# Half-row matmuls in pairs and a new order of pieces for the softmax maxima of a cross-attention

## The chip, the cores and the metric

The kernel runs on one core of a Trainium2 chip. The metric is the device time of one execution in microseconds (us). Five engines work side by side and meet at semaphores: TensorE (PE in the profile; its weight loads, PEld, overlap its matmuls), the vector engine (DVE), ScalarE (ACT), GpSimd (POOL), and SyncE (SP), whose queue issues the transfers.

## The reference

A decoder layer for 32 batches of 56 tokens of width 128: a self-attention whose softmax runs over the queries, a cross-attention to 1500 context rows of width 96 per batch, and a mixture of 8 experts with the two best chosen per token. Each part is followed by a residual sum and a layer norm. The change lies in the cross-attention:

```
q = (query @ Wq + bq)  -> 16 heads of 8
k = (key_value @ Wk + bk), v = (key_value @ Wv + bv)
attn = softmax(clip(q @ k^T * 8**-0.5, -10000, 10000))     # 16 heads x 56 queries x 1500 keys
x = (attn @ v) @ Wo + bo
```

## The kernel before, in words

The self-attention and the setup take the first 70 us or so, then a loop over the 32 batches does the cross-attention, and from some 768 us on the experts run. The change touches the loop and the part ahead of it that prepares batches 0 and 1.

**One batch in the loop.** The scores are computed transposed: keys in the partitions, 896 = 16 x 56 columns of head and query in the free dimension. The 1500 keys are cut into 12 chunks of 125, and the loop has one slot c per chunk (`period`, lines 1576 to 1665 for TensorE, 998 to 1063 for the vector engine, 748 to 778 for ScalarE). In a slot TensorE makes the scores of chunk c (line 1590: 4 matmuls into banks 2 and 3 or 4 and 5), ScalarE takes their exponentials (line 759), and TensorE later multiplies these by the values into bank 6 (lines 1655 and 1659: 4 + 4 matmuls with 25 and 9 columns of weights, at partitions 0, 32, 64 and 96 of the output; each matmul of plain fp32 leaves two records). `OUTPUTS` names the slots in which the outputs of which chunks are made: 2 in slot 2, 3 in slots 5 and 8, 1 in slot 10, 3 in slot 11.

**The maxima.** A softmax needs the maximum over all keys of each row before the first exponential. It is made one or two batches ahead, from rounded keys `K_hi` and block-diagonal queries `Q_bd` (head h has its 8 rows 8h to 8h+7, and zeros in the others). Rows of 16 heads x 56 queries make 7 groups of 128 (RG = 7), the keys 3 thirds of 500 (NB = 3): 21 *pieces* per batch, each one matmul of 128 rows, 128 columns of weights and 500 columns (`piece`, line 1403, matmul at 1414) into bank 0 or 1 by `bank_of(n)`, and one maximum over 500 numbers by the vector engine (`piece_max`, line 941, at 946). Piece n is group n // 3, third n % 3. With two banks, piece n waits until piece n - 2 is reduced (line 1413). When all 21 are done, `row_max` (954) takes the maximum of the three thirds, TensorE turns it into a row (`turn`, 1431, slot 8), `row_out` (961) writes its negative, and SyncE's queue moves it into the last row of the next batch's stacked queries.

**The order.** It is written out by hand in tables from slot to pieces: `EARLY_PIECES` stand right behind the slot's scores, `MID_PIECES` behind the projections of slot c and ahead of the outputs, `LATE_PIECES` behind the outputs. Pieces 0 to 8 belong to the batch after next, 9 to 20 to the next (`pieces`, line 328). The vector engine takes early and mid pieces first in a slot, then `row_max` in slot 7, `row_out` in slot 8, the reciprocals of the softmax sums in slots 0 and 1 (line 1013), the scaling of the outputs in slot 5 (line 1018), then late pieces. In TensorE's queue a slot holds: scores, early pieces, the sums of the batch before (slot 0, line 1545), a third of the values of a later batch (slots 9, 11 and 3, line 1421), a third of its keys (slots 5, 6 and 8, line 1426), mid pieces, the turn (slot 8), outputs, late pieces. Each engine runs its queue strictly in the order written; ahead of the loop the pieces of batch 0 and the first 9 of batch 1 are listed by `pieces0` and `pieces1`.

Of the kernel before, what the change touches and what calls it, by code (L numbers as in the profile page):

```python
# [24 lines left out]
AX = mybir.AxisListType  # L25
# [14 lines left out]
KB = 500  # L40
NB = NK // KB
# [12 lines left out]
SUM_SLOT, TURN_SLOT = 0, 8  # L54
V_COPIES = (9, 11, 3)
K_COPIES = (4, 6, 7)
EARLY_PIECES = {0: (9,), 1: (10,), 2: (11,), 3: (12,), 4: (14,), 6: (18,), 7: (20,), 9: (2,), 10: (4,), 11: (6,)}
MID_PIECES = {3: (13,), 5: (15, 16), 6: (19,), 8: (0,), 9: (3,), 11: (7,)}
LATE_PIECES = {5: (17,), 8: (1,), 10: (5,), 11: (8,)}
OUTPUTS = {2: (0, 1), 5: (2, 3, 4), 8: (5, 6, 7), 10: (8,), 11: (9, 10, 11)}  # L60
NP = 3
P_AT, T_AT, X_AT, LOGITS_AT = 3, 5, 9, 11
# [6 lines left out]
RG = HQ // 128  # L69
HG = H // 4  # L70
PIECES = RG * NB
SUM = 0
V3, V1 = 3 * DH + 1, DH + 1
VC = 4 * (V3 + V1)
# [2 lines left out]
PRIME = 4  # L77
# [8 lines left out]
def decoder_kernel(nc, gate_rows, x1_rows, xT, x, ctx_in, wq, wk, wv, xWq, xbq, xWk, xbk, xWv, xbv, xWo, xbo, Wr, W1, W2, out):  # L86
    stack = ExitStack()

    def sb(name, shape, dt=F32):
        return stack.enter_context(nc.sbuf_tensor(name, shape, dt))  # L90

    def sem(name):
        return stack.enter_context(nc.semaphore(name))

    with stack:
# [30 lines left out]
        K_hi = sb("K_hi", [128, 2, NK], F32R)  # L126
        K_st = sb("K_st", [128, 2, HG, NK], F32R)
        Q_st = sb("Q_st", [DC + 1, 2, HG, 4, S], F32R)
        Q_bd = sb("Q_bd", [128, 2, H, S], F32R)
# [9 lines left out]
        def at(parts, *shape, place=None):  # L139
            n = math.prod(shape)  # L140
            o = used[0]
            used[0] += n
            place = whole if place is None else place
            assert used[0] <= place.shape[-1], used[0]
            v = place[0:parts, o:o + n]
            if len(shape) == 2:
                v = v.rearrange("p (a b) -> p a b", b=shape[1])
            elif len(shape) == 3:
                v = v.rearrange("p (a b c) -> p a b c", b=shape[1], c=shape[2])
            return v  # L150

        Qs_all = at(DC, HG, B * S)
        start = used[0]
# [22 lines left out]
        def held(u):  # L176
# [15 lines left out]
        mx = at(128, RG, NB)  # L192
# [107 lines left out]
        F = {n: sem("f_" + n) for n in (  # L300
            "keys_made", "keys_copied", "keys_high", "keys_low",
            "values_made", "values_copied", "queries_spread", "stacked_spread", "max_scores_made",
            "piece_max_taken", "row_max_taken", "extremes_kept", "max_transposed", "max_row_ready",
            "scores_made", "weights_ready", "outputs_made", "outputs_copied", "sums_spread", "sums_inverted",
            "outputs_scaled", "ones_ready", "bank_cleared", "bad_ready", "bad_summed",
            "flag_ready")}
# [25 lines left out]
        def bank_of(n):  # L332

            return bank[0 if n == 0 else (n + 1) % 2]

        def has(b, ahead):

            return not isinstance(b, int) or 0 <= b + ahead < B
# [116 lines left out]
        def _(pool):  # L455
# [3 lines left out]
            def step(ins):  # L459
                ended[0] += 1  # L460
                ins.then_inc(pool_step, 1)
                pool.wait_ge(pool_step, ended[0])

            def keep(t, pattern, base, mult, op=ALU.is_ge, fill=0.0):
                step(g.affine_select(out=t, in_=t, pattern=pattern, compare_op=op, fill=fill, base=base,
                                     channel_multiplier=mult))
# [12 lines left out]
            for par in range(2):  # L479
                step(g.memset(V2[par][:, :, 0:4 * V3].rearrange("p c (m r) -> p c m r", r=V3)[:, :, :, SUM], 1.0))  # L480
                step(g.memset(V2[par][:, :, 4 * V3:VC].rearrange("p c (m r) -> p c m r", r=V1)[:, :, :, SUM], 1.0))
            for s in range(SLOTS - 1):
# [7 lines left out]
            for a3 in range(3):  # L490
                step(g.tensor_copy(four_heads[32 * a3:32 * a3 + 32, :], head_rows[32 * a3:32 * a3 + 32, 4 * a3:4 * a3 + 4]))
            keep(sum_rows[:].rearrange("p (g c) -> p g c", c=32), [[-32, 4], [0, 32]], -SUM, 1, ALU.not_equal, 1.0)
            pool.sem_inc(consts, 1)
# [3 lines left out]
            def later_constants():  # L497
# [18 lines left out]
                for g4 in range(4):  # L516
                    keep(sum_row[:], [[0, 1]], -SUM - 32 * g4, 1, ALU.not_equal, 1.0)
                pool.sem_inc(consts, 1)
# [14 lines left out]
            def spread_queries(b, par):  # L533

                g.tensor_tensor(Q_bd[:, par], Qt_all[:, bass.ds(b * S, S)].unsqueeze(1).to_broadcast([128, H, S]),  # L535
                                head_rows[:].unsqueeze(2).to_broadcast([128, H, S]), ALU.mult).then_inc(F["queries_spread"], 1)
# [33 lines left out]
            def period(b, par, half):  # L570
                if has(b, 2):
                    pool.wait_ge(F["max_scores_made"], (b + 1) * PIECES + PRIME)
                    spread_queries(b + 2, par)
# [64 lines left out]
        def _(act):  # L638
# [109 lines left out]
            def period(b, par, half):  # L748
                for c in range(NC):
# [13 lines left out]
                    if c in K_COPIES and has(b, 2):  # L763
                        n = K_COPIES.index(c)
                        act.wait_ge(F["max_scores_made"], (b + 1) * PIECES + PRIME)
                        act.wait_ge(D_[f"khi{par}"], (half + 1) * (16 * 2 * HG))
# [81 lines left out]
        def _(dve):  # L848
            v = nc.vector
# [43 lines left out]
            def first_attended(n):  # L893

                dve.wait_ge(X_[n], 16)
                dve.wait_ge(S1["outputs_made"], n + 1)
                y = firsts[n].xq
                for t in range(QT):
                    last = v.scalar_tensor_tensor(y[:, t, :], bank[2 + n % 2][0:TT, D * t:D * t + D], quads3[n].ri[:, t:t + 1], y[:, t, :], ALU.mult, ALU.add)
                last.then_inc(S1["residual_added"], 1)  # L900
                dve.wait_ge(S1["residual_added"], n + 1)
                statistics(S1, quads3[n], lambda t: y[:, t, :], tie(0), True)
# [38 lines left out]
            def piece_max(b, n):  # L941

                dve.wait_ge(F["max_scores_made"], b * PIECES + n + 1 + PRIME)
                if n == 0 and (not isinstance(b, int) or b >= 1):
                    dve.wait_ge(F["row_max_taken"], b + PRIME)
                v.reduce_max(mx[:, n // NB, n % NB:n % NB + 1], bank_of(n)[:, 0:KB], AX.X).then_inc(F["piece_max_taken"], 1)  # L946

            def row_max(b):

                dve.wait_ge(F["piece_max_taken"], (b + 1) * PIECES + PRIME)  # L950
                if not isinstance(b, int) or b >= 1:
# [23 lines left out]
            for n in range(8):  # L975
                piece_max(0, n)
            first_attended(3)
            for n in range(8, PIECES):
                piece_max(0, n)
            row_max(0)  # L980
            row_out(0)
            for n in range(3):
                piece_max(1, n)
# [14 lines left out]
            def period(b, par, half):  # L998
                for c in range(NC):
                    taken(b, c, EARLY_PIECES)  # L1000
                    taken(b, c, MID_PIECES)
                    if c == 7 and has(b, 1):
# [11 lines left out]
                    if c == 5 and has(b, -1):  # L1014
                        dve.wait_ge(F["sums_inverted"], 2 * b + PRIME)
                        if isinstance(b, int) and b == 1:
                            dve.wait_ge(D_["qr"], 16 * 3 * HG)
                        v.scalar_tensor_tensor(OS_all[:, :, bass.ds((b - 1) * S, S)], O_sb.rearrange("p (s q) -> p s q", s=SLOTS), 1.0,
                                               R_sb.rearrange("p (s q) -> p s q", s=SLOTS), ALU.mult, ALU.mult, accum_out=chk_all[:, bass.ds(b - 1, 1)]).then_inc(F["outputs_scaled"], 1)
                    taken(b, c, LATE_PIECES)  # L1020
                    P, norms = passes[0], passes[0].base3["rstd_ready"]
# [245 lines left out]
            with dve.If(clamped > 0):  # L1267
# [8 lines left out]
                with dve.Fori(0, B) as i:  # L1276
# [6 lines left out]
                    for j in range(G2):  # L1283
                        n = i * G2 + j
# [48 lines left out]
        def _(pe):  # L1333
            t_ = nc.tensor
            mm = t_.matmul
# [67 lines left out]
            def piece(b, par, n, turns):  # L1403

                if n == 0:
                    pe.wait_ge(F["queries_spread"], b + 1 + PRIME)
                if n < NB:
                    pe.wait_ge(F["keys_high"], b * NB + n + 1 + PRIME)
                if n == 2:
                    if turns:  # L1410
                        pe.wait_ge(F["max_row_ready"], b + PRIME)
                elif not (isinstance(b, int) and b == 0 and n == 0):
                    pe.wait_ge(F["piece_max_taken"], b * PIECES + (1 if n == 1 else n - 1) + PRIME)
                mm(bank_of(n)[:, 0:KB], Q_bd[:, par].rearrange("p h q -> p (h q)")[:, 128 * (n // NB):128 * (n // NB) + 128],  # L1414
                   K_hi[:, par, (n % NB) * KB:(n % NB) * KB + KB], start=True, stop=True).then_inc(F["max_scores_made"], 1)

            def value_project(par, n):

# [157 lines left out]
            def period(b, par, half):  # L1576
                for c in range(NC):
# [15 lines left out]

                    max_scores(b, par, c, EARLY_PIECES)
                    if c == SUM_SLOT and has(b, -1) and has(b, 0):
# [37 lines left out]
                    if c in K_SLOTS and has(b, 2):  # L1633
# [6 lines left out]
                        key_project(par, n, bank[7])  # L1640
                    max_scores(b, par, c, MID_PIECES)
                    if c == TURN_SLOT and has(b, 1):
                        turn(b + 1)
                    if has(b, 0):
                        for k in OUTPUTS.get(c, ()):
# [15 lines left out]
                            last.then_inc(F["outputs_made"], 1)  # L1661
                    max_scores(b, par, c, LATE_PIECES)
                    if isinstance(b, int) and b == B - 2 and c == 8:
# [83 lines left out]
            with pe.If(clamped > 0):  # L1747
                pe.wait_ge(second, 1)
                with pe.Fori(0, B) as i:
# [13 lines left out]
                    for j in range(G2):  # L1763
                        n = i * G2 + j
                        pe.wait_ge(S2["max_ready"], n + PRIME)
                        for c in range(NB):
                            last = mm(bank[c][0:TT, 0:KB], Qbd[:, 2 * j:2 * j + 2, :].rearrange("p h q -> p (h q)"), KT[:, KB * c:KB * c + KB],
                                      start=True, stop=True)
# [94 lines left out]
```

## Time and profile before

| | |
|---|---|
| median of 3 runs | 981.94 us (979.5 to 982.6) |
| span of the profiled execution | 981.2 us (the page gives no other time of that execution) |
| TensorE busy | 934.3 us (95%) |
| vector engine busy | 737.5 us (75%) |
| ScalarE busy | 647.0 us (66%) |
| GpSimd busy | 350.3 us (36%) |
| mean granted TensorE clock | 0.978 of full speed |

The rows further down are lines of the profile's page and of questions to its trace. A line of a group of instructions has the line of the kernel (L1414), the engine, the operation, output <- inputs, shapes and count, then busy time, mean duration and the idle time ahead with what ended it. A line of the chain or the timeline begins with its start and its length in us.

### The profile page before, as it was taken

To read this page: it belongs to the slowest core of one execution; us is meant where nothing else is said; L and a number is where in the kernel's file an instruction comes from. 1 tells how busy PE (TensorE), PEld (TensorE's weight loads), DVE (VectorE), ACT (ScalarE), POOL (GpSimd) and SP (SyncE) were. 2 spreads that over 40 slices of the span, in tenths; PEclk is the share of its full clock that TensorE was granted. 3 is DMA by queue.
4 is the path that set the end of the run, shared out by engine and by line. 5 is a ranking of instruction groups with operands and counts; after the bars stand their busy time and mean duration, and the time that the engine had idled before them with its cause. 6 is when DMAs were issued, how large, how long until landed. Compare 5 with 4: busy or idle time off the path is not lost.

```text
span 981.2 us, 28874 instructions
## 1 busy us (share of the span) xinstructions
PE 934.3 (95%) x10535; PEld 753.6 (77%) x10535; DVE 737.5 (75%) x1426; ACT 647.0 (66%) x1081; POOL 350.3 (36%) x334
## 2 busy tenths in 40 slices
PE   6877999999999999999999999999999899999995
PEld 4645787877777777787777877778777678999894
DVE  6673777777777777777777777777788857777996
ACT  3654777777777777777777777777776444445554
POOL 6452352223233332222323333222231413112992
PEclk8897999999999999999999999999999899999998
DMA  6538566666555556666655555666654201002331
GB/s 140 116 75 197 119 143 135 145 136 138 131 118 118 118 125 138 140 136 137 136 128 118 118 118 128 140 138 137 138 121 96 66 1 44 23 22 83 130 113 41
DMA packets 43626, 111.45 MB, mean 114 GB/s; under 512 B 15491, under 2 KB 26053, under 8 KB 43461
## 3 DMA queue, kind: packets, MB, share of 16 engines
q1 hardware_dynamic: 43572, 110.77, 49.9%
q8 instruction: 30, 0.49, 0.2%
q14 instruction: 24, 0.19, 0.1%
HBM read 32.23 MB, written 1.89 MB: 35 GB/s over the span
## 4 chain that ended last, share of the span: by engine, by line
PE 90%; DVE 4%; ACT 2%; SPq 2%; issue 1%; DMA 1%; POOL 0%; ACTq 0%; DVEq 0%
PE psum L1590 18%; PE psum L1414 18%; PE psum L1655 13%; PE psum L1421 8%; PE psum L1426 8%; PE psum L1659 4%; PE psum L1682 3%; PE psum L1683 2%; PE psum L1684 2%; PE psum L1695 2%; PE psum L1694 2%; PE psum L1696 2%; PE psum L1545 1%; PE psum L1431 1%; SPq L395 1%
## 5 line engine op out<-in xcount | busy, mean ns | idle before, releaser
L946 DVE TENSOR_REDUCE arena<-psum 128x1 f32<-128x500 f32 x672 | 443.0, 671 | 176.9 <-PE psum L1414 176.7
L759 ACT ACTIVATE arena<-psum 125x896 f32<-125x896 f32 x384 | 348.1, 916 | 114.2 <-PE psum L1590 102.5
L1414 PE MATMUL psum<-K_hi,Q_bd 128*128 128x500 f32 x672 | 310.0, 470 | 7.0 <-DVE arena L946 4.2
L547 POOL TENSOR_TENSOR arena<-arena,K_hi 128x500 fp32r<-128x500 f32 x96 | 119.9, 1249 | 407.3 <-ACT K_hi L690 407.3
L1590 PE MATMUL psum<-Q_st,K_st 97*125 97x224 f32 x1536 | 243.7, 281 | 0.7 <-ACT arena L759 0.6
L1590 PEld LDWEIGHTS psum<-Q_st,K_st 97*125 97x125 f32 x1536 | 222.7, 190 | 23.1 <-issue 3.9
L1414 PEld LDWEIGHTS psum<-K_hi,Q_bd 128*128 128x128 f32 x672 | 128.2, 191 | 64.9 <-issue 27.1
L1655 PE MATMUL psum<-arena 125*25 125x168 f32 x3072 | 171.2, 313 | 0.2
L813 ACT ACTIVATE K_st<-psum 128x448 fp32r<-128x448 f32 x128 | 69.7, 544 | 79.2 <-PE psum L1684 77.7
L1659 PE MATMUL psum<-arena 125*9 125x56 f32 x3072 | 117.7, 214 | 0.0
L1659 PEld LDWEIGHTS psum<-arena 125*9 125x9 f32 x3072 | 94.5, 92 | 16.7
L1426 PE MATMUL psum<-arena,WkA 97*128 97x500 f32 x192 | 99.0, 597 | 7.3 <-ACT arena L688 7.2
L1421 PEld LDWEIGHTS psum<-WvA,arena 97*125 97x125 f32 x768 | 99.8, 189 | 3.8
L1421 PE MATMUL psum<-WvA,arena 97*125 97x128 f32 x768 | 100.4, 274 | 0.0
L1655 PEld LDWEIGHTS psum<-arena 125*25 125x25 f32 x3072 | 69.5, 104 | 34.1 <-issue 32.9
L1071 DVE SCALAR_TENSOR_TENSOR K_st<-psum,K_st 128x448 fp32r<-128x448 f32 x128 | 76.8, 615 | 12.2 <-ACT K_st L813 11.5
L688 ACT COPY arena<-psum 128x500 f32<-128x500 f32 x96 | 55.5, 578 | 44.8 <-PE psum L1426 34.9
L540 POOL TENSOR_TENSOR Q_st<-arena,four_heads 96x896 fp32r<-96x896 f32 x32 | 53.7, 1677 | 55.4 <-PE psum L1590 55.4
L703 ACT COPY arena<-psum 125x384 f32<-125x384 f32 x96 | 46.6, 486 | 33.9 <-PE psum L1421 33.9
L690 ACT CAST K_hi<-arena 128x500 fp32r<-128x500 f32 x96 | 58.5, 610 | 3.1
L1013 DVE RECIPROCAL arena<-psum 128x112 f32<-128x112 f32 x64 | 53.8, 842 | 1.4 <-PE psum L1545 1.4
L535 POOL TENSOR_TENSOR Q_bd<-Qt_all,head_rows 128x896 fp32r<-128x896 f32 x32 | 54.1, 1690 | 0.5 <-PE psum L1414 0.5
(250 smaller groups left out, 1052.4 us busy)
## 6 DMA issues: line engine op xcount, KB each, us to landing
K_st<-K_hi SPq DMA_DIRECT2D x256, 187.5 KB, 4.7
K_st<-arena SPq DMA_DIRECT2D x128, 187.5 KB, 3.4
arena<-in_ctx SPq DMA_DIRECT2D x32, 562.5 KB, 6.7
arena<-gate_rows SPq DMA_DIRECT2D x8, 896.0 KB, 4.4
arena<-in_L_ffn_W SPq DMA_DIRECT2D x16, 256.0 KB, 3.1
Q_st<-max_row SPq DMA_DIRECT2D x224, 0.5 KB, 1.7
arena<-OS_all SPq DMA_DIRECT2D x12, 168.0 KB, 4.1
x_rows<-x_all SPq DMA_DIRECT2D x1, 896.0 KB, 6.5
```

What stands on the lines that cost most here:

```text
L547: g.tensor_tensor(low.bitcast(F32R), low, K_hi[:, par, n * KB:n * KB + KB].bitcast(F32), ALU.subtract).then_inc(F["keys_low"], 1)
L690: a.copy(K_hi[:, par, n * KB:n * KB + KB], K_lo[:, n * KB:n * KB + KB]).then_inc(F["keys_high"], 1)
L759: a.activation(P2[c % NP].rearrange("p (n k) -> p n k", n=2), psum[0:CK, 2 + 2 * (c % 2):4 + 2 * (c % 2), 0:HQ // 2], ACT.Exp)\
L813: a.activation(h_hi[u % 2][:, f], bank[f][:, 0:QC], ACT.Relu).then_inc(S4["hidden_high"], 1)
L946: v.reduce_max(mx[:, n // NB, n % NB:n % NB + 1], bank_of(n)[:, 0:KB], AX.X).then_inc(F["piece_max_taken"], 1)
L1071: v.scalar_tensor_tensor(h_lo[k % 2][:, f], bank[f][:, 0:QC], 0.0, h_hi[k % 2][:, f].bitcast(F32), ALU.max, ALU.subtract)\
L1414: mm(bank_of(n)[:, 0:KB], Q_bd[:, par].rearrange("p h q -> p (h q)")[:, 128 * (n // NB):128 * (n // NB) + 128], K_hi[:, par, (n % NB) * KB ...
L1421: last = mm(bank[7][0:CK, 128 * k:128 * k + 128], ctxT2[:, par, CK * q:CK * q + CK], WvA[:], start=True, stop=True)
L1426: mm(into[:, 0:KB], WkA[:], ctxT2[:, par, n * KB:n * KB + KB], start=True, stop=True).then_inc(F["keys_made"], 1)
L1590: last = mm(bank[2 + 2 * (c % 2) + g // 2][0:CK, 4 * S * (g % 2):4 * S * (g % 2) + 4 * S], K_st[0:DC + 1, par, g, c * CK:c * CK + CK], Q_s ...
L1655: mm(bank[6][32 * m:32 * m + V3, 0:3 * S], values[:, k, V3 * m:V3 * m + V3], weights_[:, 3 * S * m:3 * S * m + 3 * S], start=(k == 0), sto ...
L1659: last = mm(bank[6][32 * m:32 * m + V1, 3 * S:4 * S], values[:, k, 4 * V3 + V1 * m:4 * V3 + V1 * m + V1], weights_[:, (12 + m) * S:(13 + m ...
```

## The change

Two things change. The pieces that need only one half of the array's rows use only that half: groups 0 to 2 have all of their heads in rows 0 to 63, groups 4 to 6 in rows 64 to 127, and group 3 lies across both and keeps all 128 rows. And the order is new: `PIECE_ORDER` goes through the thirds of the keys one after the other, within a third a lower and an upper half follow each other, and the slot tables put most pieces in twos right behind the scores. For the pieces of groups 0 to 2 and 4 to 6 the pairs that stand next to each other in the loop are 1 and 2, 3 and 4, 5 and 6, 7 and 8, 9 and 10, 11 and 12, 14 and 15, 16 and 17, 18 and 19; the whole-array pieces 0, 13 and 20 stand alone. A pair's two matmuls write banks 0 and 1. The wait for a third of the keys moves to the first piece of the third.

```diff
-EARLY_PIECES = {0: (9,), 1: (10,), 2: (11,), 3: (12,), 4: (14,), 6: (18,), 7: (20,), 9: (2,), 10: (4,), 11: (6,)}
-MID_PIECES = {3: (13,), 5: (15, 16), 6: (19,), 8: (0,), 9: (3,), 11: (7,)}
-LATE_PIECES = {5: (17,), 8: (1,), 10: (5,), 11: (8,)}
+EARLY_PIECES = {0: (9, 10), 1: (11, 12), 2: (13,), 3: (14, 15), 4: (16, 17), 6: (18, 19), 7: (20,), 9: (3, 4), 10: (5, 6), 11: (7, 8)}
+MID_PIECES = {8: (0,)}
+LATE_PIECES = {8: (1, 2)}
...
+HALF = 64
+PIECE_ORDER = ((3, 0), (0, 0), (4, 0), (1, 0), (5, 0), (2, 0), (6, 0),
+               (0, 1), (4, 1), (1, 1), (5, 1), (2, 1), (6, 1), (3, 1),
+               (0, 2), (4, 2), (1, 2), (5, 2), (2, 2), (6, 2), (3, 2))
...
-                v.reduce_max(mx[:, n // NB, n % NB:n % NB + 1], bank_of(n)[:, 0:KB], AX.X).then_inc(F["piece_max_taken"], 1)
+                j, third = PIECE_ORDER[n]
+                v.reduce_max(mx[:, j, third:third + 1], bank_of(n)[:, 0:KB], AX.X).then_inc(F["piece_max_taken"], 1)
...
-                if n < NB:
-                    pe.wait_ge(F["keys_high"], b * NB + n + 1 + PRIME)
+                j, third = PIECE_ORDER[n]
+                if n % RG == 0:
+                    pe.wait_ge(F["keys_high"], b * NB + third + 1 + PRIME)
...
-                mm(bank_of(n)[:, 0:KB], Q_bd[:, par].rearrange("p h q -> p (h q)")[:, 128 * (n // NB):128 * (n // NB) + 128],
-                   K_hi[:, par, (n % NB) * KB:(n % NB) * KB + KB], start=True, stop=True).then_inc(F["max_scores_made"], 1)
+                rows = slice(0, 128) if j == RG // 2 else slice(0, HALF) if j < RG // 2 else slice(HALF, 128)
+                mm(bank_of(n)[:, 0:KB], Q_bd[rows, par].rearrange("p h q -> p (h q)")[:, 128 * j:128 * j + 128],
+                   K_hi[rows, par, third * KB:third * KB + KB], start=True, stop=True).then_inc(F["max_scores_made"], 1)
```

## Rows read from the trace of the kernel before

**Rows 1.** The page: busy time of the engines, and the chain by engine.

```profile
PE 934.3 (95%) x10535; PEld 753.6 (77%) x10535; DVE 737.5 (75%) x1426; ACT 647.0 (66%) x1081; POOL 350.3 (36%) x334
...
PE 90%; DVE 4%; ACT 2%; SPq 2%; issue 1%; DMA 1%; POOL 0%; ACTq 0%; DVEq 0%
```

**Rows 2.** Windows: stretch and length in us, busy us, granted clock, DMA share, GB/s.

```profile
0.00:100.00 100.00, 73.23 (x488) 53.62 (x488) 61.31 (x139) 51.38 (x119) 46.31 (x62) 0.88 0.58 130
102.59:747.66 645.07, 645.07 (x8556) 509.71 (x8555) 491.64 (x790) 478.51 (x755) 210.45 (x194) 1.00 0.60 129
768.00:981.00 213.00, 194.00 (x1175) 173.29 (x1167) 165.37 (x448) 104.56 (x190) 91.68 (x77) 0.96 0.19 60
```

**Rows 3.** The chain of waits in order of time, from one period of the loop.

```profile
396.75 0.43 PE psum L1590 x4
397.18 0.23 PE psum L1414
...
400.05 0.28 PE psum L1655 x8
400.43 0.42 PE psum L1414
...
402.36 0.32 PE psum L1414
...
407.41 0.87 PE psum L1421 x8
...
409.18 0.42 PE psum L1655 x8
...
414.24 0.38 PE psum L1545 x2
```

**Rows 4.** The timeline of the same period: pieces and reductions, reciprocals, loads of outputs.

```profile
401.46 2.60 DVE L946 TENSOR_REDUCE arena<-psum 128x1 f32<-128x500 f32 x4
...
402.18 0.19 PEld L1414 LDWEIGHTS psum<-K_hi,Q_bd 128*128 128x128 f32 x1 [0.64 <-DVE arena L946]
402.18 0.49 PE L1414 MATMUL psum<-K_hi,Q_bd 128*128 128x500 f32 x1
...
409.10 0.15 PEld L1655 LDWEIGHTS psum<-arena 125*25 125x25 f32 x8 [0.23 <-issue]
...
413.61 1.34 DVE L946 TENSOR_REDUCE arena<-psum 128x1 f32<-128x500 f32 x2 [1.02 <-PE psum L1414]
...
414.88 0.85 DVE L1013 RECIPROCAL arena<-psum 128x112 f32<-128x112 f32 x1
...
415.64 0.61 DVE L946 TENSOR_REDUCE arena<-psum 128x1 f32<-128x500 f32 x1
...
416.17 0.84 DVE L1013 RECIPROCAL arena<-psum 128x112 f32<-128x112 f32 x1
...
417.40 0.40 PE L1414 MATMUL psum<-K_hi,Q_bd 128*128 128x500 f32 x1
...
417.83 0.68 DVE L946 TENSOR_REDUCE arena<-psum 128x1 f32<-128x500 f32 x1 [0.28 <-PE psum L1414]
```

**Rows 5.** The page's costliest groups: reductions of the maxima, loads of the outputs.

```profile
L946 DVE TENSOR_REDUCE arena<-psum 128x1 f32<-128x500 f32 x672 | 443.0, 671 | 176.9 <-PE psum L1414 176.7
...
L1655 PEld LDWEIGHTS psum<-arena 125*25 125x25 f32 x3072 | 69.5, 104 | 34.1 <-issue 32.9
```

**Rows 6.** Timeline and one window: TensorE's waits ahead of the loop and in batch 0.

```profile
50.23 1.08 PE L1414 MATMUL psum<-K_hi,Q_bd 128*128 128x500 f32 x2 [0.80 <-DVE arena L946]
...
87.46 2.04 PE L1426 MATMUL psum<-arena,WkA 97*128 97x500 f32 x2 [7.17 <-ACT arena L688]
...
87.00:90.00 3.00, 2.54 (x5) 1.46 (x6) 0.05 (x1) 2.97 (x5) 1.24 (x1) 0.50 1.08 214
```

## The prediction

> **What bounds the kernel.** I read the page's busy times and chain first. TensorE is busy for 95% of the span and holds 90% of the chain that ended last, the vector engine 4% [rows 1]. Then the windows, to see where that holds. Between 102.59 and 747.66 us TensorE has no idle time at all and the clock is granted in full; in the first 100 us it is busy for 73 us, and the change touches nothing behind 768 us [rows 2]. That stretch is 29 periods of the batch loop (the two ends are the sums of two batches, 29 batches apart), so a period takes 645.07 / 29 = 22.24 us, with 21 pieces in it. The vector engine is busy there for 491.64 of 645.07 us, 16.95 us a period: not the bound, but three quarters full. It has only two banks of maxima to work from, and every piece waits until the piece two before it has been reduced.
>
> Then the chain inside one period, which gives prices as the path paid them [rows 3]. A piece between full-array matmuls costs 0.23 us. The same piece behind the column-tiled output matmuls (25 and 9 columns wide) costs 0.42, so going from tiles to the whole array costs 0.19. Eight records of the first output behind a full-array matmul cost 0.42 where eight later ones cost 0.28: 0.14 into tiles. Scores of a slot cost 0.43, the sums 0.38, one output in all 400.43 - 400.05 = 0.38.
>
> Last the timeline, for how a piece and its maximum hand over to each other [rows 4]. A piece starts at 417.40 and its reduction at 417.83: 0.43 later. Two reductions in a row take 1.34, so 0.67 each, which is also the mean over all 672 [rows 5]. The first of four reductions in 2.60 us ends at 401.46 + 0.65 = 402.11, and the waiting piece's load starts at 402.18; its matmul lasts 0.49 where one with its load hidden lasts 0.40. Hand-back is thus 0.07 + 0.09, say 0.17 with rounding.
>
> **The change, part by part.** *Half the rows.* 18 of the 21 pieces of a batch now use one half of the rows, and nine times a period a lower and an upper half follow each other, into the two banks. The trace has no such pair. The nearest rows are the four column tiles of the outputs: eight records of 168 columns take 0.28 us, where eight records of 128 columns on the whole array take 0.87 [rows 3], which would be 0.87 x 168 / 128 = 1.14. Tiles do run side by side, and their eight loads, 104 ns each [rows 5], are over in 0.15 us [rows 4], so the loads overlap too. Bounds of a pair's saving: nothing (no overlap), and 0.23 - 0.02 = 0.21 (the second half 0.02 behind the first). I take 0.21, as the tiles' rows are close to complete overlap: 9 x 0.21 = **-1.89 us**.
>
> *Entering and leaving half-row mode.* Pairs stand between full-array scores, keys, values and sums. Seven (slots 0, 1, 3, 4, 6, 9, 11) have two new changes each; the pair of slot 10 stands ahead of outputs and adds one, the late one of slot 8 stands behind outputs and adds one. That is 16 a period. Price of one: from nothing, if halves of the rows count as the whole array, to 0.19, what leaving column tiles costs [rows 3]. I take 0.19, because the half-row matmul is as much another cut of the array as the column tile is: 16 x 0.19 = **+3.04 us**.
>
> The Trainium skill says of this, in "TensorEngine Tiling (Array Packing)", Key Properties, that a change of tiling mode, as against a change of tile within one mode, drains the engine. The column tiles' rows agree with it; no row here shows it for halves of the rows. By this rule the sum stands as I make it, without it the 3.04 falls away (the second rival).
>
> *The order.* Before, slots 0 to 4 hold single pieces (9, 10, 11, 12 and 13, 14); now they hold 9 and 10, 11 and 12, 13, 14 and 15, 16 and 17. Slots 0 and 1 also hold the two reciprocals, 0.85 each, which stand between the reductions in the vector engine's queue [rows 4]. A waiting piece holds up all of TensorE's queue. Stretch by stretch, counted from a piece's start:
> - Piece 13 needs 11 reduced. Vector engine: 0.43 + 0.67 (9) + 0.67 (10) + 0.85 + 0.67 (11) + 0.17 = 3.46. TensorE's own work: pair 0.25, change 0.19, sums 0.38, scores 0.43, change 0.19, pair 0.25, change 0.19, scores 0.43 = 2.31. Wait 1.15.
> - Piece 15 needs 13 reduced, and ahead of it stand 12 and the second reciprocal. 13 starts when 11 is done, 0.17 later; from there 0.67 + 0.85 + 0.67 = 2.19, 2.02 past 13's start, and 0.17 to hand back: 2.19. TensorE: 13 0.23, into outputs 0.14, two outputs 0.76, change 0.19, scores 0.43, change 0.19, piece 14 0.02 = 1.96. Wait 0.23.
> - Pieces 1 and 2 now follow the outputs of slot 8, and 3 and 4 come one score group later. 3 needs 1 reduced: 0.43 + 0.67 + 0.17 = 1.27, against 0.25 + 0.19 + 0.43 + 0.19 = 1.06: wait 0.21. 4 needs 2 reduced, 0.67 later, against 0.02: wait 0.65.
> - Elsewhere (16 and 17, 5 to 8, 18 and 19) projections or outputs lie between and cover the reductions; no wait.
>
> Sum **+2.24 us** of waits. These are not there before: the piece shown waiting at 402.18 [rows 4] cost the chain 0.32 instead of 0.23 [rows 3], and that 0.09 is saved, since the vector engine no longer has four reductions queued there. The other waits of the table (a third of the keys is now waited for at pieces 0, 7 and 14 in place of 0, 1 and 2) cost nothing: those keys are copied slots earlier.
>
> A period: -1.89 + 3.04 + 2.24 - 0.09 = +3.30 us; 29 periods 95.7. The period of the first batch (70 to 102 us) is held up by a 7.17 us idle time of TensorE on the keys [rows 6], so only its last four slots count: 6 changes 1.14, four pairs -0.84, waits 0.86, about +1.2. The last period with pieces has slots 0 to 7 alone: ten changes 1.90, five pairs -1.05, waits 1.38, less 0.09: +2.1. Ahead of the loop pieces wait for reductions anyway (0.80 at 50 us [rows 6]); bounds there 0 and some 10 us (26 halves with two changes of 0.19 each), I take 1, as TensorE is idle for 27 of those 100 us [rows 2]. Sum: 95.7 + 1.2 + 2.1 + 1 = 100. The page gives 981.2 us as the profiled span and no time of that execution beside it; the median of the runs is 0.7 above it. 981.9 + 100 = **1082 us**.
>
> The waits are all under 1.2 us. Behind a 7.17 us idle time the granted clock is 0.50, the lower of its levels [rows 6]; the stretch that holds the 0.64 us wait keeps the full clock [rows 2, 4]. I count nothing for the clock.
>
> **Rivals.**
> - *Changes cost, halves don't overlap*, so the change doesn't do what it is built for. Nothing saved; the longer TensorE work hides more of the waits: 0.73 + 0 + 0.44 = 1.17. 3.04 + 1.17 - 0.09 = 4.1 a period, 119 in 29, 5 at the ends: 1106. Against it speaks the overlap of column tiles. 0.13.
> - *Halves overlap, changes are free.* TensorE reaches the waits sooner: 1.72 + 0.42 + 0.59 + 0.65 = 3.4. -1.89 + 3.4 - 0.09 = 1.4 a period: 1024. For it: the output columns' width, not the rows, is what the shown tiles differ in. 0.16.
> - *Neither*: full price, free changes, the order alone. Waits 1.30 + 0.2 + 0.38 + 0.44 = 2.3, so 2.2 a period: 1049. 0.12.
> - *The other side*: a waiting piece doesn't hold up TensorE's queue, so the scores behind it fill the time. The waits cost nothing, and with free changes -1.89 - 0.09 = -2.0 a period: 924. It decides once waits fall under 1.98 us a period with free changes; with priced changes even no wait leaves +1.1. Against it: TensorE idles on a reduction at 50 us with other work queued [rows 6]. 0.05, and 0.03 that terms cancel to no change.
>
> **How the numbers follow.** My forecast has 0.51. The range takes it and the three slower rivals: from just under 1024 to a few us past 1106, 1020 to 1112; for the likeliest case alone it is 1070 to 1095 (second half's start and price per change). Left out: the other side, a cancelled sum, and prices per change above those of column tiles. A measurement tells about 0.3% from no change, as the runs spread by 0.3%. Faster 0.05, same 0.03, slower 0.92.
>
> **What would show it.** In the profile after: piece matmuls of 64 rows starting within some 0.02 us of each other in pairs; 0.42 in place of 0.23 in the chain for the matmul behind a pair; idle time of TensorE ended by the line of the maxima at pieces 13, 3 and 4, some 1.1 and 0.9 us a period; a period of 25.5 us. If scores follow a pair at 0.23, the change price is wrong; if pair members start 0.2 apart, the overlap is; if the period is under 22.2, the waits are.

## The result and the profile after

The changed kernel takes 1071.74 us (median of 4 runs, 1066.46 to 1074.99) against 982.27 us before: ratio 1.0924, 95% interval 1.089 to 1.0958. It is slower by some 89 us; forecast were 100 us, 1082 us in all.

The page of the changed kernel, busy times and the chain by engine (the rows that answer to [rows 1]):

```profile
PE 1017.1 (95%) x10535; PEld 747.7 (70%) x10535; DVE 693.4 (65%) x1426; ACT 640.1 (60%) x1081; POOL 350.5 (33%) x334
...
PE 82%; DVE 10%; issue 5%; ACT 2%; DVEq 0%; DMA 0%; SPq 0%; POOL 0%; ACTq 0%
```

TensorE is still busy for 95% of the span, now of a longer one, so its busy share alone says nothing. The chain does: the vector engine has gone from 4% to 10%, and "issue", time in which an engine waited for nothing that the profile shows, from 1% to 5%. No engine has got more matmuls, weight loads or vector instructions to do: the counts are the same.

Where the time lies in the span, by the sums of the batches, which stand at the head of each period (timeline of the changed kernel: start, length):

```profile
110.31 0.65 PE L1552 MATMUL psum<-arena,sum_rows 128*128 128x224 f32 x2
...
837.06 0.65 PE L1552 MATMUL psum<-arena,sum_rows 128*128 128x224 f32 x2
```

The same 29 periods that took 645.07 us [rows 2] take 837.06 - 110.31 = 726.75: 25.06 us each against 22.24, +2.82 a period and 81.7 us in all. The part ahead of them takes 110.3 instead of 102.6 us, +7.7. Behind them the span is 0.9 us shorter. 81.7 + 7.7 - 0.9 = 88.5, which is the difference of the two spans (1069.7 - 981.2).

Inside a period, the chain of waits of the changed kernel in order of time (answers to [rows 3]):

```profile
415.68 0.43 PE psum L1421 x2
416.11 1.07 PE psum L1428 x8
417.18 0.43 PE psum L1597 x4
417.61 0.43 PE psum L1421 x2
418.04 0.63 PE psum L1597 x4
418.66 0.84 PE psum L1433 x2
...
457.05 0.70 PE psum L1421 x2
```

Both pieces of a pair together cost 0.43 us of the chain, where one whole-array piece costs 0.23. Read as the theory has it, the second is all but free, and the first carries 0.20 for entering half-row mode; the runs below without overlap and without pairs test that reading. What follows a pair is dearer by the same: scores 0.63 instead of 0.43, a third of the values 1.07 instead of 0.87. A pair with both changes costs 0.43 + 0.20 = 0.63, two single pieces cost 0.46. The last line is the pair 7 and 8 of slot 11: it costs 0.70, for a reason that the timeline shows.

The timeline around slots 0 to 2, then of the whole-array piece 20, of slots 8 and 9, and of slots 10 and 11 (answers to [rows 4]): loads, pieces, reductions, reciprocals.

```profile
435.75 0.19 PEld L1421 LDWEIGHTS psum<-K_hi,Q_bd 64*128 64x128 f32 x2
435.75 0.49 PE L1421 MATMUL psum<-K_hi,Q_bd 64*128 64x500 f32 x2
436.27 1.26 DVE L951 TENSOR_REDUCE arena<-psum 128x1 f32<-128x500 f32 x2 [2.70 <-PE psum L1421]
437.17 0.90 PE L1421 MATMUL psum<-K_hi,Q_bd 64*128 64x500 f32 x2
437.45 0.85 DVE L1018 RECIPROCAL arena<-psum 128x112 f32<-128x112 f32 x1
437.59 0.18 PEld L1421 LDWEIGHTS psum<-K_hi,Q_bd 64*128 64x128 f32 x1 [0.23 <-DVE arena L951]
438.21 1.19 DVE L951 TENSOR_REDUCE arena<-psum 128x1 f32<-128x500 f32 x2
438.88 0.19 PEld L1421 LDWEIGHTS psum<-K_hi,Q_bd 128*128 128x128 f32 x1 [0.37 <-DVE arena L951]
...
448.25 0.19 PEld L1421 LDWEIGHTS psum<-K_hi,Q_bd 128*128 128x128 f32 x1
...
448.35 0.40 PE L1421 MATMUL psum<-K_hi,Q_bd 128*128 128x500 f32 x1
...
452.18 2.52 DVE L951 TENSOR_REDUCE arena<-psum 128x1 f32<-128x500 f32 x4 [0.94 <-PE psum L1421]
...
452.91 0.18 PEld L1421 LDWEIGHTS psum<-K_hi,Q_bd 64*128 64x128 f32 x1 [0.33 <-DVE arena L951]
...
453.50 0.18 PEld L1421 LDWEIGHTS psum<-K_hi,Q_bd 64*128 64x128 f32 x1 [0.40 <-DVE arena L951]
...
455.94 1.26 DVE L951 TENSOR_REDUCE arena<-psum 128x1 f32<-128x500 f32 x2 [1.24 <-PE psum L1421]
...
456.98 0.77 PE L1421 MATMUL psum<-K_hi,Q_bd 64*128 64x500 f32 x2
...
457.26 0.18 PEld L1421 LDWEIGHTS psum<-K_hi,Q_bd 64*128 64x128 f32 x1
```

Where nothing waits, two half-row matmuls take 0.49 us together and their two loads 0.19, both as long as one alone: they run side by side. But piece 12's load stands until 437.59 and piece 13's until 438.88, the latter 3.13 us behind piece 9 (TensorE's own work in between, by the prediction's sum: 2.31). Pieces 3 and 4 wait at 452.91 and 453.50. Each is released by the reduction of the piece two before. Piece 8 must wait for piece 6 in the same way. The profile names no releaser there, but the times fit: the reductions of 5 and 6 end at 455.94 + 1.26 = 457.20, and the load of 8 stands until 457.26, 0.28 behind piece 7 at 456.98. That is the 0.70 instead of 0.43.

The timeline also shows part of what a change consists of. The load of the whole-array piece 20, between full-array matmuls, starts 0.10 ahead of its matmul, and the matmul lasts 0.40; the loads of the pair at 435.75 start together with its matmuls, which last 0.49. So about half of the 0.20 is a weight load that is no longer hidden; what the rest is, these rows don't show.

### The profile page after: what moved, and what is told of

It reads as the page before. It is cut to its first block, busy times and chain, and to the rows that moved or that the text cites. A ratio compares the mean times of both kernels' runs of the same rounds, so it can differ in the third digit from the quotient of the medians.

```text
span 1069.7 us, 28849 instructions
## 1 busy us (share of the span) xinstructions
PE 1017.1 (95%) x10535; PEld 747.7 (70%) x10535; DVE 693.4 (65%) x1426; ACT 640.1 (60%) x1081; POOL 350.5 (33%) x334
## 3 DMA queue, kind: packets, MB, share of 16 engines
HBM read 32.23 MB, written 1.89 MB: 32 GB/s over the span
## 4 chain that ended last, share of the span: by engine, by line
PE 82%; DVE 10%; issue 5%; ACT 2%; DVEq 0%; DMA 0%; SPq 0%; POOL 0%; ACTq 0%
PE psum L1597 15%; PE psum L1421 15%; PE psum L1662 12%; PE psum L1428 10%; PE psum L1433 8%; DVE arena L951 6%; PE psum L1666 4%; PE psum L1689 3%; PE psum L1690 2%; PE psum L1702 2%; PE psum L1691 2%; PE psum L1701 2%; PE psum L1703 2%; DVE arena L1018 1%; PE psum L1552 1%
## 5 line engine op out<-in xcount | busy, mean ns | idle before, releaser
L951 DVE TENSOR_REDUCE arena<-psum 128x1 f32<-128x500 f32 x672 | 425.2, 668 | 311.2 <-PE psum L1421 311.0
L1597 PE MATMUL psum<-Q_st,K_st 97*125 97x224 f32 x1536 | 277.2, 304 | 3.4 <-issue 2.8
L1421 PE MATMUL psum<-K_hi,Q_bd 64*128 64x500 f32 (+1 forms) x672 | 238.5, 511 | 17.6 <-DVE arena L951 7.9
L1597 PEld LDWEIGHTS psum<-Q_st,K_st 97*125 97x125 f32 x1536 | 207.5, 191 | 56.1 <-issue 41.5
L1421 PEld LDWEIGHTS psum<-K_hi,Q_bd 64*128 64x128 f32 (+1 forms) x672 | 91.4, 188 | 91.0 <-DVE arena L951 46.8
L1428 PE MATMUL psum<-WvA,arena 97*125 97x128 f32 x768 | 113.8, 293 | 0.0
L1428 PEld LDWEIGHTS psum<-WvA,arena 97*125 97x125 f32 x768 | 95.1, 194 | 23.5 <-issue 23.5
L1433 PE MATMUL psum<-arena,WkA 97*128 97x500 f32 x192 | 103.2, 620 | 0.1
```

What stands on the lines that cost most here:

```text
L951: v.reduce_max(mx[:, j, third:third + 1], bank_of(n)[:, 0:KB], AX.X).then_inc(F["piece_max_taken"], 1)
L1421: mm(bank_of(n)[:, 0:KB], Q_bd[rows, par].rearrange("p h q -> p (h q)")[:, 128 * j:128 * j + 128], K_hi[rows, par, third * KB:third * KB + ...
L1428: last = mm(bank[7][0:CK, 128 * k:128 * k + 128], ctxT2[:, par, CK * q:CK * q + CK], WvA[:], start=True, stop=True)
L1433: mm(into[:, 0:KB], WkA[:], ctxT2[:, par, n * KB:n * KB + KB], start=True, stop=True).then_inc(F["keys_made"], 1)
L1597: last = mm(bank[2 + 2 * (c % 2) + g // 2][0:CK, 4 * S * (g % 2):4 * S * (g % 2) + 4 * S], K_st[0:DC + 1, par, g, c * CK:c * CK + CK], Q_s ...
```

## The experiments

The theory after the result had three terms per period: 16 changes of the array's cut at 0.20 us, nine overlaps of 0.21, and waits on the reductions. The rival put all on the changes, or all on the order.

**Order alone.** Every piece on all rows:

```diff
-                rows = slice(0, 128) if j == RG // 2 else slice(0, HALF) if j < RG // 2 else slice(HALF, 128)
+                rows = slice(0, 128)
```

> The new order and slot tables with every piece on all 128 rows: the order alone. Theory (changes of the array's cut 3.2 us, waits 1.6 us, overlap -1.9 us a period): only the waits are left, about 0.97 at piece 13 and 0.7 at pieces 3 and 4, less 0.09: +1.6 us a period, 46 in 29 periods, 1026 to 1032 us, period 23.8 us, and the clock ahead of the loop as in the kernel before. Rival, the loss is all from leaving and entering half-row mode: 982 us. Rival, the prices of the prediction for the order alone: 1049 us.

Measured: 1027.95 us, ratio 1.047 (1.0414 to 1.0526). Timeline of this run, the sums of the same two batches, and the wait of piece 13:

```profile
102.03 0.54 PE L1552 MATMUL psum<-arena,sum_rows 128*128 128x224 f32 x2
...
438.47 0.19 PEld L1421 LDWEIGHTS psum<-K_hi,Q_bd 128*128 128x128 f32 x1 [0.56 <-DVE arena L951]
...
793.84 0.54 PE L1552 MATMUL psum<-arena,sum_rows 128*128 128x224 f32 x2
```

(793.84 - 102.03) / 29 = 23.86 us, +1.62. About half of the whole loss is the order, with no half row in it. Both rivals fall.

**Pairs without overlap.** The same places and changes, but both pieces of a pair in the lower half:

```diff
-                rows = slice(0, 128) if j == RG // 2 else slice(0, HALF) if j < RG // 2 else slice(HALF, 128)
+                rows = slice(0, 128) if j == RG // 2 else slice(0, HALF)
```

> As the changed kernel, but both pieces of a pair use the lower half of the rows, so the number of matmuls, the changes of mode, the order and the waits' places stay and only running side by side is taken away. The maxima of head groups 4 to 6 are left out by this (they are read as zero). Theory (a pair overlaps and saves some 0.2 us): nine pairs 1.8 us a period longer, of which about 0.6 is hidden in the waits at pieces 13, 3 and 4: +1.2 us, 35 in 29 periods, 1100 to 1112 us; second matmul some 0.2 us behind the first. Rival, pairs don't overlap in the changed kernel either: 1072 us.

Measured: 1104.37 us, ratio 1.122 (1.1155 to 1.1286). The chain of this run, a pair between scores, then the first and last sums of the 29 periods:

```profile
437.94 0.65 PE psum L1421 x2
438.59 0.63 PE psum L1597 x4
```
```profile
120.50 0.65 PE L1552 MATMUL psum<-arena,sum_rows 128*128 128x224 f32 x2
...
871.95 0.65 PE L1552 MATMUL psum<-arena,sum_rows 128*128 128x224 f32 x2
```

A pair costs 0.65 instead of 0.43: the overlap is real and worth 0.22. The time came out where expected, but its parts did not quite: a period takes (871.95 - 120.50) / 29 = 25.91, +0.85 against the changed kernel and not +1.2. Of 9 x 0.22 = 2.0 us some 1.1 vanish in waits: the pair 7 and 8, for one, costs 0.65 here too, so that piece 8 no longer waits. Ahead of the loop 10 us more are lost, at a lower clock (last section).

**Half rows in the old order.** The tables and piece numbers of before, each piece on its half:

```diff
...
+                j = n // NB
+                rows = slice(0, 128) if j == RG // 2 else slice(0, 64) if j < RG // 2 else slice(64, 128)
...
```

> The order and slots of the kernel before, but each piece of groups 0 to 2 and 4 to 6 on its half of the rows: no pairs of opposite halves, 26 new changes between half-row and other matmuls in a period, the reductions where they were. Theory (0.20 us for each change): +5.2 us a period, 151 in 29 periods, with the part ahead of the loop some 5 more: 1130 to 1142 us. Rival, a change is half as dear and the waits cost more: about 1060 us. Rival, changes are free: 982 us.

Measured: 1131.11 us, ratio 1.1515 (1.1454 to 1.1576). The chain of this run (single half-row pieces and the scores behind them), and its sums:

```profile
441.38 0.43 PE psum L1416
441.80 0.62 PE psum L1592 x4
```
```profile
111.14 0.54 PE L1547 MATMUL psum<-arena,sum_rows 128*128 128x224 f32 x2
...
894.67 0.54 PE L1547 MATMUL psum<-arena,sum_rows 128*128 128x224 f32 x2
```

(894.67 - 111.14) / 29 = 27.02, +4.78 over before for 26 changes: 0.18 each on average, against 0.20 read from the chain. A half-row piece alone costs 0.43, as much as a pair in the changed kernel, so 0.20 of the pair's 0.43 is the entry. The "half as dear" rival falls. The time is in the stated range, but again its parts are not as stated: 4.78 a period instead of 5.2, and 111.14 - 102.59 = 8.6 us ahead of the loop instead of some 5.

**Whole rows ahead of the loop.** The pieces of `pieces0` and `pieces1` on all rows, the loop as changed:

```diff
-            def piece(b, par, n, turns):
+            def piece(b, par, n, turns, whole=False):
...
-                rows = slice(0, 128) if j == RG // 2 else slice(0, HALF) if j < RG // 2 else slice(HALF, 128)
+                rows = slice(0, 128) if whole or j == RG // 2 else slice(0, HALF) if j < RG // 2 else slice(HALF, 128)
...
-                    piece(0, 0, n, False)
+                    piece(0, 0, n, False, True)
...
-                    piece(1, 1, n, True)
+                    piece(1, 1, n, True, True)
```

> As the changed kernel, but the pieces ahead of the loop use all 128 rows; inside the loop nothing differs. The first 110.3 us of the changed kernel (up to the sums of the first batch) took 102.6 before, and the granted clock there is 0.77 against 0.88. Theory, the lower clock comes with half-row matmuls ahead of the loop: these 7.7 us come back, 1063 to 1066 us, clock of the first 100 us 0.86 to 0.90. Rival, it comes from the new order and its waits: 1072 us. Rival, half-row matmuls of the first batch of the loop alone keep the clock low from 70 to 96 us: 1067 to 1070 us.

Measured: 1063.87 us, ratio 1.0831 (1.0766 to 1.0896); the interval touches that of the changed kernel, so the runs alone don't part them, but the traces do. Windows of this run, then of the changed kernel, then of the kernel before (stretch, length, TensorE busy and its count, the other engines, then granted clock, DMA share and GB/s):

```profile
0.00:100.00 100.00, 74.90 (x479) 52.33 (x479) 61.54 (x139) 50.52 (x118) 45.58 (x61) 0.88 0.57 130
45.00:70.00 25.00, 19.09 (x88) 11.72 (x88) 18.65 (x44) 13.36 (x30) 13.14 (x11) 1.00 0.32 78
70.00:97.00 27.00, 21.77 (x197) 14.09 (x197) 10.71 (x19) 13.02 (x20) 5.38 (x4) 0.81 0.87 193
```
```profile
0.00:100.00 100.00, 83.39 (x408) 54.88 (x412) 56.38 (x132) 46.65 (x112) 42.60 (x59) 0.74 0.56 129
45.00:70.00 25.00, 22.23 (x74) 11.87 (x74) 15.31 (x38) 12.08 (x26) 12.33 (x11) 0.77 0.23 53
70.00:97.00 27.00, 26.65 (x151) 17.58 (x149) 10.93 (x20) 9.46 (x15) 2.07 (x2) 0.52 0.96 217
```
```profile
45.00:70.00 25.00, 19.08 (x88) 11.64 (x88) 18.50 (x44) 12.73 (x28) 13.11 (x11) 1.00 0.28 65
70.00:97.00 27.00, 19.72 (x212) 14.98 (x211) 11.06 (x18) 13.68 (x22) 4.96 (x4) 0.81 0.93 209
```

The sums of this run's first batch:

```profile
104.18 0.65 PE L1552 MATMUL psum<-arena,sum_rows 128*128 128x224 f32 x2
```

The clock is back at that of before in both stretches, and the first sums stand at 104.2 us in place of 110.3: 6.1 of the 7.7 us. The order, which this run keeps, isn't their cause, and neither are the half-row matmuls of the loop's first batch, which it keeps too.

**Pairs spread out.** Only the tables change, so that projections or outputs lie between a pair and the next:

```diff
+EARLY_PIECES = {4: (13,), 7: (19, 20)}
+MID_PIECES = {0: (9, 10), 2: (11, 12), 5: (15, 16), 8: (0,), 10: (3, 4), 11: (5, 6)}
+LATE_PIECES = {4: (14,), 5: (17, 18), 8: (1, 2), 11: (7, 8)}
```

> The changed kernel with other slot tables alone: pairs stand behind projections or outputs, so that reductions are done before the next pair needs its bank, and most pairs stand at a place where TensorE changes its cut anyway. Theory: waits of 1.6 us a period fall to some 0.2, 13 new changes in place of 16 (2.6 us), eight pairs overlap (-1.7): +1.1 us a period against the kernel before, 32 in 29 periods, and the 7.7 us ahead of the loop stay: 1018 to 1027 us, period 23.3 us. Rival, the waits only hid what would be lost otherwise, and three changes fewer are all of the gain: 1050 to 1056 us.

Measured: 1023.87 us, ratio 1.0452 (1.0419 to 1.0485). The sums of this run:

```profile
106.78 0.55 PE L1552 MATMUL psum<-arena,sum_rows 128*128 128x224 f32 x2
...
787.51 0.55 PE L1552 MATMUL psum<-arena,sum_rows 128*128 128x224 f32 x2
```

(787.51 - 106.78) / 29 = 23.47 us, +1.23 over before and 1.59 under the changed kernel: 48 us are won back with the same matmuls. Three changes fewer and one overlap less make up 3 x 0.20 - 0.22 = 0.4 of the 1.59; the rest, 1.2, is by difference what the waits gave back. They were lost time, and didn't hide the changes. Ahead of the loop, 106.78 - 102.59 = 4.2 us are lost and not the 7.7 that I expected to stay.

**The same tables, whole rows.**

```diff
-                rows = slice(0, 128) if j == RG // 2 else slice(0, HALF) if j < RG // 2 else slice(HALF, 128)
+                rows = slice(0, 128)
```

> The same tables with all pieces on 128 rows: neither changes of mode, nor overlap, and few waits. Theory: nothing is left of the loss, 978 to 988 us, period 22.1 to 22.5 us, the first 100 us at a clock near 0.88. Rival, the order by thirds itself costs something that isn't a wait (the orders' places of keys and projections): over 995 us.

Measured: 986.35 us, ratio 1.0065 (1.004 to 1.009). Its period is (752.81 - 100.84) / 29 = 22.48 us, +0.24. Little of the loss is left (the interval lies just clear of no change); going through the keys by thirds costs at most that, apart from the places of the pieces. What the 0.24 are isn't shown.

```profile
100.84 0.55 PE L1552 MATMUL psum<-arena,sum_rows 128*128 128x224 f32 x2
...
752.81 0.55 PE L1552 MATMUL psum<-arena,sum_rows 128*128 128x224 f32 x2
```

**Six pairs, one change each.** The tables above, half rows only for six pairs that stand on one side of the outputs (3 and 4 in slot 10 would have been a seventh), whole rows ahead of the loop:

```diff
+SIX = (1, 2, 5, 6, 7, 8, 11, 12, 15, 16, 17, 18)
...
+                rows = slice(0, 128) if whole or n not in SIX else slice(0, HALF) if j < RG // 2 else slice(HALF, 128)
...
```

> The same tables; half rows for the six pairs alone that add one change each (1 and 2, 5 and 6, 7 and 8, 11 and 12, 15 and 16, 17 and 18), whole rows ahead of the loop. Theory: a pair's overlap (0.21) and one change (0.20) cancel, so the time is that of the same tables with whole rows within 0.5%, period within 0.15 us. Rival, a change beside the column tiles is free as the engine changes there anyway: 1.2 us a period faster, 35 us, some 945 us. Rival, a pair's overlap is not worth 0.2 us: up to 35 us slower.

Measured: 991.69 us, ratio 1.0127 (1.0097 to 1.0157). The sums of this run:

```profile
99.69 0.55 PE L1553 MATMUL psum<-arena,sum_rows 128*128 128x224 f32 x2
...
754.94 0.55 PE L1553 MATMUL psum<-arena,sum_rows 128*128 128x224 f32 x2
```

(754.94 - 99.69) / 29 = 22.59 us, 0.11 more than with whole rows. The period is as expected; the median is 0.54% above that of the whole rows, a little past the 0.5% that I gave. One change eats up one overlap: even at its best place a pair wins nothing here. The rival that a change beside the column tiles is free falls. The one that an overlap isn't worth 0.2 us falls in full size: six pairs that lose their overlap would lose some 1.2 us a period, and 0.11 is 0.02 for each. No version tried beats the kernel before.

## Why the prediction was right

By its own steps:
- *Direction and size.* 1082 us against 1071.74, in the range; 3.30 us a period against 2.82.
- *Half the rows, -1.89 us.* Right. The columns' tiles were the right neighbour: 0.43 for a pair, 0.65 without overlap, so 0.22 each.
- *Entering and leaving, +3.04 us.* Right: 0.20 in the chain, 0.18 from the 26 changes, 0.19 taken. The Trainium skill says that a change of tiling mode drains the engine ("TensorEngine Tiling (Array Packing)", Key Properties). These runs agree with it for halves of the rows as far as they show that each change costs time; that the engine drains they don't show by itself.
- *The order, +2.24 us of waits.* The mechanism is right, and the order alone shows it; the sizes aren't. Read from the timeline: piece 13 starts 3.13 us behind piece 9 and not 3.46, so it costs 0.82 and not 1.15; pieces 3 and 4 cost 0.20 + 0.57; piece 15 waits for nothing (0.23 forecast); and piece 8, which the prediction put at nothing because outputs "lie between and cover the reductions", costs 0.70 - 0.43 = 0.27. Together 1.86. From piece 9 to the load of 13 the timeline has 0.52 us to the first reduction, 1.18 to the reciprocal, 0.76 to the reduction of 11 and 0.67 for it with the hand-back, where 0.43, 1.34, 0.85 and 0.84 were forecast. So the failed term is 0.67 for a reduction in a row: four in a row take 2.52 here, 0.63 each, and the reciprocal begins at 437.45, 0.08 before the two reductions ahead of it end at 437.53. The hand-back was too dear as well: the load of 12 starts 0.06 behind that end, and 0.17 was taken. For piece 8 it is the overlap that failed: outputs and scores don't cover the two reductions.
- *The sum of a period.* With 0.20 for a change, 3.20 - 1.89 + 1.86 - 0.09 = 3.08; with 0.18, 2.88 - 1.89 + 1.86 - 0.09 = 2.76. The 2.82 measured lies between the two, so the terms close to within what the price of a change is known to.
- *Ahead of the loop and batch 0, +2.2 us.* Wrong, +7.7 measured. The step "I count nothing for the clock" failed: I asked only whether the new waits would lower it, and not whether the half-row matmuls would. With whole rows ahead of the loop and the clock of before, 104.18 - 102.59 = 1.6 us are left.
- *The last batch with pieces, +2.1.* It takes 859.44 - 837.06 = 22.38 us instead of 768.70 - 747.66 = 21.04, +1.3. That the part behind the 29 periods is 0.9 shorter all the same comes from the batch behind it, which has no pieces at all. Windows of that batch, before and then changed:

```profile
768.70:793.81 25.11, 21.44 (x279) 17.39 (x278) 14.38 (x32) 11.24 (x13) 8.36 (x8) 0.80 0.21 62
```
```profile
859.44:882.17 22.73, 18.96 (x280) 15.74 (x279) 14.50 (x32) 11.25 (x13) 8.38 (x8) 0.92 0.21 65
```

It is 2.4 us shorter with the same work, at a granted clock of 0.92 instead of 0.80. Why the clock is higher there is not shown.

The errors have opposite signs: the periods came out 0.48 us lower than forecast (14 us in 29, most of it the waits), the end 3.0 us lower, the start 5.5 us higher, and within the waits piece 8 makes good much of what piece 13 was too dear. So the sum looks better than its terms, and that much of it is luck. The rivals without the price of a change, 1024 and 1049, and the one without overlap, 1106, are ruled out as explanations of the changed kernel by the pair's 0.43, which becomes 0.65 when the overlap is taken away, by the 0.43 of a half-row piece alone and by the 0.63 behind either; that the rest of TensorE's queue runs on past a waiting piece is ruled out by the 1.62 us of the order alone.

## What to carry to other kernels

A pair of half-row matmuls that stands between full-array matmuls saves one matmul and pays for two changes of the array's cut: here 0.22 us against 0.40. By these prices, and as an estimate only, two overlaps in a row would about carry both changes (0.44 against 0.40); no run here tried that, and with two banks the third and fourth piece would wait for reductions of 0.63 us each. And before single pieces are put in twos, count what the engine that empties the banks has in its queue at that place: 1.6 us a period, half of the loss, came from pieces that waited for reductions (about 0.8 of the changed kernel's waits stand behind a reciprocal), and most of it went away with a change of the tables alone.

## What was not expected of the hardware

Half-row matmuls went along with a lower granted clock ahead of the loop, though TensorE's busy time is longer there (fewer matmuls, each of them longer at the lower clock). From 45 to 70 us the clock is 1.00 before (TensorE busy for 19.08 us of 25) and with whole rows ahead of the loop (19.09); it is 0.77 in the changed kernel, with 22.23 us busy. With pairs in one half it is 0.50, the lower of the two levels throughout, and with halves in the old order, which has no pairs of opposite halves, 0.64:

```profile
45.00:70.00 25.00, 24.61 (x50) 11.71 (x50) 13.00 (x33) 10.89 (x23) 7.59 (x8) 0.50 0.20 49
```
```profile
45.00:70.00 25.00, 22.51 (x55) 10.87 (x55) 13.66 (x34) 11.96 (x26) 11.32 (x10) 0.64 0.20 48
```

All nine traces go this way: in this stretch the clock is 1.00 in the five with whole rows ahead of the loop, and 0.50 to 0.77 in the four with half rows there. From 70 to 97 us the changed kernel stays at 0.52 with TensorE busy for 26.65 of 27 us. So a TensorE that is busy in the trace need not have the full clock. Inside the 29 periods, with the same pairs, the clock is 1.00 (window of the changed kernel):

```profile
110.31:837.06 726.75, 711.69 (x8557) 499.15 (x8555) 448.89 (x789) 471.53 (x755) 210.47 (x194) 1.00 0.53 115
```

Whether it is the half-used array or the drains between its cuts that lowered the clock stays open: the run with whole rows ahead of the loop takes away both at once. The pairs in one half have as many changes as the changed kernel and a lower clock still, which speaks against the drains as the only cause.

Second, the overlap is close to complete also for the weight loads: two loads of opposite halves take 0.19 us together, as one does. The Trainium skill ("TensorE: Matmul & The Clock Gate", Part 3: Packing small matmuls) says that matmuls on different row groups start some 4 ns apart. The 0.49 us of two together, as long as one, agrees with that as far as the 0.01 us to which these rows are given can tell.
